# VectorE's order at the start of the first layer: half 0's features and first mask between two parts of the state space weights

## The reference

```
# first sublayer: q, k, v = split(x @ w_attn)
q = elu(q) + 1 ; k = elu(k) + 1                      # the "features"
S_t = S_(t-1) + k_t v_t^T ; z_t = z_(t-1) + k_t
y_t = (q_t S_t) / (q_t . z_t + 1e-6)
x = layernorm(x + y @ w_proj)
# second sublayer holds a state space convolution (64 modes):
dtA = exp(log_dt) * (A_re + i A_im)
dC  = C * (exp(dtA) - 1) / A                         # the "weights"
K   = 2 Re( sum_n dC_n * exp(dtA_n * l) ), l = 0..511  # the taps
```

## Time and profile before

| | |
|---|---|
| runs shown | 670.03, 669.6 and 674.61 us, median 670.03 |
| the profiled execution | 671.23 us |
| its span, first to last instruction | 669.4 us |
| busy in the span | PE 492.3, DVE 438.0, ACT 258.7, POOL 207.8 us |
| mean granted clock of TensorE | 0.851 |
| first block ends on DVE (last row of line 203) | 100.16 us |

### The profile page before, as it was taken

One profiled execution on the slowest core, in us unless ns is written; L12 is line 12 of the kernel. 1 busy time (PEld: TensorE's weight loads), 2 busy tenths in 40 slices (PEclk: granted clock), 3 DMA queues, 4 the chain that ended last, 5 costly groups with the idle time before them and its releaser, 6 DMA issues. The chain is left out here.

```text
span 669.4 us, 11535 instructions
## 1 busy us (share of the span) xinstructions
PE 492.3 (74%) x4041; PEld 357.1 (53%) x4041; DVE 438.0 (65%) x1422; ACT 258.7 (39%) x625; POOL 207.8 (31%) x245
## 2 busy tenths in 40 slices
PE   4597537473599776987768577978598889899960
PEld 2265423361577555776645466756277646455530
DVE  4569896999844777655574998895678554133225
ACT  4499702120013433654113636452266232133321
POOL 3224000553723002655010532330374037044440
PEclk9679955777899886998987677989889879999995
DMA  8100006010000031660000000000735001500012
GB/s 277 43 3 2 1 0 252 9 26 2 0 1 1 0 83 41 114 142 1 1 0 1 2 1 1 1 1 2 290 144 134 2 5 55 138 28 32 29 39 91
DMA packets 28195, 33.44 MB, mean 50 GB/s; under 512 B 5176, under 2 KB 21288, under 8 KB 27625
## 3 DMA queue, kind: packets, MB, share of 16 engines
q1 hardware_dynamic: 26204, 29.24, 14.9%
q0 software_dynamic: 1504, 3.15, 1.4%
q10 hardware_dynamic: 432, 0.33, 0.2%
HBM read 26.50 MB, written 6.21 MB: 49 GB/s over the span
## 5 line engine op out<-in xcount | busy, mean ns | idle before, releaser
L3305 DVE TENSOR_TENSOR em_inner<-banks,em_soft 128x256 f32<-128x256 f32 x31 | 13.1, 424 | 52.5 <-ACT em_soft L3141 52.5
L1777 POOL TENSOR_TENSOR ea_scaled_rows<-ea_scaled_rows 128x768 f32<-128x768 f32 (+2 forms) x24 | 27.7, 1155 | 61.6 <-ACT ea_scaled_rows L1704 60.3
L3189 POOL DMA_INDIRECT em_results<-em_y_slot,slot_rows x31 | 29.7, 957 | 49.7 <-DVE em_y_slot L3313 48.8
L219 ACT ACTIVATE norm_log<-norm_var 128x4 f32<-128x4 f32 x20 | 4.1, 205 | 85.6 <-DVE norm_var L197 85.5
L3079 PE MATMUL banks<-em_up,em_slotT 128*128 x62 | 34.9, 645 | 0.0
L1704 ACT ACTIVATE ea_scaled_rows<-banks,ea_gate 128x192 f32<-128x192 f32 x64 | 23.4, 419 | 25.5 <-PE banks L38 25.4
L2343 POOL TENSOR_TENSOR ga_to_end<-ga_cum 128x512 f32<-128x512 f32 x8 | 12.4, 1545 | 65.1 <-DVE ga_cum L2399 65.0
L1207 POOL TENSOR_TENSOR xa_prob<-xa_score,xa_top 128x308 f32<-128x308 f32 x8 | 5.6, 703 | 75.9 <-DVE xa_left L1304 75.9
L3141 ACT ACTIVATE em_soft<-banks 128x256 f32<-128x256 f32 x31 | 11.9, 383 | 42.7 <-PE banks L3079 42.7
L579 POOL TENSOR_TENSOR lin_q_strip<-lin_qT,lin_strip_head 128x512 f32<-128x512 f32 x8 | 13.9, 1741 | 43.6 <-PE banks L461 29.9
L2738 POOL TENSOR_TENSOR ca_prob<-ca_prob,ca_most 128x1232 f32<-128x1232 f32 x8 | 18.0, 2247 | 19.6 <-DVE ca_most L2791 19.6
(11 more groups left out here) (508 smaller groups left out, 1543.3 us busy)
## 6 DMA issues: line engine op xcount, KB each, us to landing
em_up<-in_em_up SPq DMA_DIRECT2D x3, 1536.0 KB, 11.3
ea_wide<-ea_gates SPq DMA_DIRECT2D x4, 1024.0 KB, 17.0
em_down<-in_em_down SPq DMA_DIRECT2D x3, 768.0 KB, 12.7
em_slots<-slot_rows SPq DMA_DIRECT2D x1, 2108.0 KB, 11.2
w_qkv<-in_w_qkv SPq DMA_DIRECT2D x1, 1536.0 KB, 7.7
slot_rows<-em_slots SPq DMA_DIRECT2D x1, 1360.0 KB, 8.1
cos_lag<-in_cos_lag SPq DMA_DIRECT2D x1, 1024.0 KB, 5.7
sin_lag<-in_sin_lag SPq DMA_DIRECT2D x1, 1024.0 KB, 8.0
```

The lines of the kernel that those rows point to most:

```text
L1777: step(pool.tensor_tensor(scaled_rows[:, k, 0:n], scaled_rows[:, k, 0:n], scaled_rows[:, k, n:2 * n], ALU.add))
L3189: pool.indirect_dma_start(core.results[:, :], bass.IndirectOffsetOnAxis(ap=slot_rows[:, s, P:P + 1].bitcast(U32), axis=0), y_slot[:, s % N ...
```

## The change

On DVE the 25 instructions of `weights` are cut in two. The first 13 (now `steps_to_weights`) stand after `strip_head` and `same_head`. Then come the four feature pieces of half 0 and `mask(0)`, then the other 12 (`weights`), then the four feature pieces of half 1. The loop over the chunks is as it was, and so are the lists of PE, ACT, POOL and SP. No instruction is added or taken away. The wait for the loads of x and the attention parameters (`wait_loaded(dve, "x", "lin")`) now stands ahead of the first 13 instructions, and `step.wait()` behind `same_head` in place of behind the last feature.

```
                 kernel.turns(dve, step)
-                kernel.weights(dve, step)
                 core.wait_loaded(dve, "x", "lin")
                 dve.tensor_reduce(strip_head[:, :], head_of[:, :].rearrange("p (r j) -> p j r", r=STRIPS), AX.X,
                                   ALU.add).then_inc(heads_ready, 1)
...
-                rows = 0
-                for n, (name, dst, _) in enumerate(features):
-                    dve.wait_ge(elu_exp, n + 1)
...
-                        rows += 1
-                        dve.wait_ge(k_rows_relu, rows)
...
                 step.wait()
+                kernel.steps_to_weights(dve, step)
+
+                def features_of(b):
+                    for n in range(4 * b, 4 * b + 4):
+                        name, dst, _ = features[n]
+                        dve.wait_ge(elu_exp, n + 1)
+                        if name[1] != "s":
+                            ring[name].taken(dve)
+                            w = 512
+                        else:
+                            dve.wait_ge(k_rows_relu, 2 * b + n % 4 - 1)
+                            w = 2 * P
+                        dve.scalar_tensor_tensor(dst, exp_of[:, n % 2, 0:w].rearrange("p (a c) -> p a c", c=P), 1.0,
+                                                 relu_of[:, n % 2, 0:w].rearrange("p (a c) -> p a c", c=P),
+                                                 ALU.min, ALU.add).then_inc(elu_done, 1)
...
+                features_of(0)
                 mask(0)
+                kernel.weights(dve, step)
+                features_of(1)
                 for g in range(NT):
...
-    def weights(self, dve, step):
+    def steps_to_weights(self, dve, step):
...
         step(dve.tensor_tensor(ni, ni, q, ALU.add))
+
+    def weights(self, dve, step):
+        are, aim = (self.t["modes"][:, n] for n in (0, 1))
+        em, cm, re, im, nr, ni, q = (self.small[n][:, :] for n in (4, 5, 6, 7, 8, 9, 1))
         step(dve.tensor_tensor(re, are, are, ALU.mult))
```

More of the change, by code:

```diff
@@ L592, in _ @@
                                               spread(head_of[:, :], 2, [P, H, D])))
-                rows = 0
-                for n, (name, dst, _) in enumerate(features):
-                    dve.wait_ge(elu_exp, n + 1)
[L596 to L599, removed]
-                        rows += 1
-                        dve.wait_ge(k_rows_relu, rows)
[L602 to L605, removed]
-                step.wait()
+                step.wait()
+                kernel.steps_to_weights(dve, step)
[12 more added lines that the diff above has]
+                                                 ALU.min, ALU.add).then_inc(elu_done, 1)
                 def mask(g):
@@ L804, in turns @@
         dve.tensor_tensor(small[1][:, :], turn, small[4][:, :], ALU.subtract).then_inc(self.small_fraction, 1)
-    def weights(self, dve, step):
+    def steps_to_weights(self, dve, step):
         dve.wait_ge(self.tanh_ready, 1)
         dve.wait_ge(self.small_sines, 2)
-        are, aim, cre, cim = (self.t["modes"][:, n] for n in range(4))
+        cre, cim = (self.t["modes"][:, n] for n in (2, 3))
         th, sin, half, em, cm, re, im, nr, ni, q = (self.small[n][:, :] for n in (0, 2, 3, 4, 5, 6, 7, 8, 9, 1))
```

## The result

| | kernel before | changed kernel |
|---|---|---|
| runs | 20, median 672.62 us (669.6 to 675.22) | 20, median 669.66 us (667.01 to 675.09) |
| ratio, 95% interval | | 0.9961 (0.9944 to 0.9978) |
| profiled execution | 671.23 us, span 669.4 | 669.62 us, span 667.8 |
| ACT's near turns start | 31.67 us | 27.91 us |
| last layernorm step of the first block ends | 100.16 us | 96.27 us |

The changed kernel is faster by 0.22 to 0.56%, which is 1.5 to 3.8 us. The medians differ by 2.96 us. The forecast was a gain of 4.5 us and a time of 665.5 us, between 661.5 and 669.5; the measured median of 669.66 lies just above that range.

The account below looks back on a forecast made before the run. ACT's unbroken run from the near turns to the first layernorm's root was taken to bound the first block. Strip and head 0, ACT's run 4.5 us earlier, DVE's surplus lost in waits: 670.03 less 4.5, 665.5 us, range 661.5 to 669.5.

Parts of the forecast that it names:

- The chain of the first block: First block: its end follows DVE's tail, ACT's root and ACT's unbroken run from the near turns at 31.67 us.
- Strips and heads ahead of the weights at no cost: DVE's start: strip_head and same_head, 0.36 us, fit into 0.93 us of idle time and cost 0.
- The end of the first score: PE, first block: score starts at 16.41 without a wait, ends at 17.55 or 18.50 us by the clock.
- the case of the end at 18.50: PE's first score at the lower clock, so that half 1's q piece can start at 25.35 us.
- The second rival: First block: a late score 0, at 20.9 us, loses the whole gain, time 670.0; chance 0.07.
- the later blocks, put at nothing on average: Behind the first block: no term in the sum, 1.5 to 2 us either way for the clock.
- the 12 instructions 18.33 - 13.76 = 4.57: DVE, first block: the second part of the weights, behind the first mask, takes 4.57 us.
- the upper case: First score at the upper clock: half 1's q piece at 24.40 us, ACT's near turns 4.78 us earlier.
- over 2 us from 569.2: From the first block's end to the span's end: a rest this far off would show the forecast wrong.
- the third rival: Later blocks' PE clock: 9 us more at the lower level use up the 4.5 us gain; chance 0.08.
- The absolute time: Whole kernel: 665.5 us, from the shown median of 670.03 less the gain of 4.5 us.
- The chances: Whole kernel: within 1% 0.84, faster by over 1% 0.13, slower by over 1% 0.03.

Follow-up runs that it names:

- the two repeats: The kernel before and the changed kernel, each run again without an edit: ratios to the kernel before 0.9986 and 0.9951.
- mask only: Kernel before with only the earlier first mask, all 25 weight instructions ahead of the features again: ratio 1.0015.
- split only: Changed kernel with only the split of the weights kept, first mask behind the features of both halves: ratio 0.989 to the kernel before.
- fourth strip later: Changed kernel with POOL's fourth strip waiting for DVE's eighth feature piece: ratio 0.9941 to the kernel before.
- the three padded ones: Changed kernel with 6, 12 or 24 dead DVE instructions behind the first block's last layernorm: ratios 0.9969, 1.0017, 1.0054 to the kernel before.
- weights late: Changed kernel with the 12 weight instructions moved into DVE's wait ahead of the first far fraction: ratio 0.9894 to the kernel before.
- the root was moved on ACT itself: Weights moved late, plus ACT's first layernorm steps between the 12th and 13th far sizes: ratios 0.9871 and 0.9856 to the kernel before.
- the one of 697.09 us: Profiled execution of the kernel before, run again without an edit: 697.09 us, left out of every ratio.
- padded with 12: Changed kernel with 12 dead DVE instructions behind the first block's last layernorm: ratio 1.0017 to the kernel before.
- the third set: Runs padded with 6 and with 24 and the fastest version again, beside the kernel before at a median of 680.76 us.
- padded with 24: Changed kernel with 24 dead DVE instructions behind the first block's last layernorm: ratio 1.0054 to the kernel before.

## Why the prediction was right and wrong

**The chain of the first block was right.** The forecast read the block's end back to ACT's near turns. In all eleven profiles in which ACT's list was untouched (before, after, the two repeats, mask only, split only, fourth strip later, the three padded ones, weights late) the last layernorm row of the block ended 68.2 to 68.5 us behind the start of the near turns (for instance 27.91 to 96.27 and 23.84 to 92.19). It broke only when the root was moved on ACT itself: 65.4 and 66.7 us. Mask only shows the same from the other side.

**Strips and heads ahead of the weights at no cost: right.** They ran at 8.07 to 8.51, and DVE still waited 0.60 us for ACT's sines.

**The end of the first score: met, but by luck.** It ended at 17.59; I had 17.55 and 18.50 as ends and took 70% of the way to the first. The way there was another. I had PE's k and v rows at the lower level to their end at 16.41 and the score behind them without a wait. The clock rose within these rows, they ended 0.9 us earlier, and the score then waited 0.92 us for the k piece that the strip held. The two cancel. I had also read the earlier trace rows wrongly: in the kernel before, the first five of the eight k and v records took 0.63 us each and the last two 0.38, so there too the clock had risen before 16.41, between 15.4 and 15.8, and 3.09 us is not the pace of the lower level throughout. In all thirteen profiles the last of these records is at the faster pace (0.38 us, 0.44 in the one of 697.09 us): none of them shows the case of the end at 18.50. The second rival, a score that starts near 20.9, is excluded by its start at 16.45. By the Trainium skill (TensorE: Matmul & The Clock Gate, Part 1: The HAM clock gate) the instant of the rise varies between runs: here the trace agrees, since the k and v rows, which began at 13.3 to 13.9 in each profile, took 3.09 us in the kernel before, 2.84 in its repeat, 2.10 after, 1.89 in the repeat of that and 3.15 in the split-only kernel.

**The terms that failed.** The forecast time was 4.2 us too low, and three terms of its sum make that up: the level that the 4.5 was taken from (2.6 us), the first block, whose end moved 3.9 us and not 4.5 (0.6 us), and the later blocks, put at nothing on average, which gave back 0.9 us of the 3.9. The mechanism of the first block held. Each of the three is taken up below.

**The step that failed in the first block: "the 12 instructions 18.33 - 13.76 = 4.57".** They took 5.41. I had used their duration from a place where POOL stood still, and had not counted that the strip of chunk 3, which used to come at 36.70 when DVE was waiting for PE, now becomes free at the end of score 1 in the midst of them. A DVE instruction with two inputs in SBUF that starts just behind a strip is held until the strip has ended. The runs with the strip moved (4.57 us again) and the split-only kernel (another strip, another instruction) show it. The sum then closes: 4.78 of the upper case, less 0.84 for the held instruction, less 0.17 because this execution's loads landed later, is 3.77, and the near turns moved by 3.76. The same hold on the k piece (1.54 us for 0.68) cost less: PE could have started the first score some 0.4 us earlier, when the strip was there (14.81 and half of 2.48 us, an estimate). The two ks pieces behind it took 1.59 us together, and the mask, at 17.83, followed them and not the score, which had ended at 17.59.

**The start of the block varies, and I had taken it as fixed.** ACT's first activation waits for the last load of the state space parameters. It began at 6.49 us in the profile before, at 6.66 in the changed one, and between 6.66 and 7.53 in the others. Everything up to the near turns shifts with it. Counted from there, the near turns come after 25.18, 25.02 and 24.72 us with all 25 weights in front (the last with the earlier mask), after 21.25, 20.85, 20.85, 20.85 and 20.95 in the changed kernel and its padded forms, 20.21 with the strip moved, 18.91 with the split alone and 17.15 to 17.21 with the weights late. So the change is worth some 4.1 us on this stretch (25.1 less 20.95, means of the two profiles before and the five after), where I had 4.5.

**The step that failed behind the first block: the later blocks give back nothing on average.** The sum has no term for them, only 1.5 to 2 us either way in the range, and no row stood behind that; my reason was that most blocks start from a standstill and replay the same sequence. The medians moved by 2.96 and 2.79 us in two sets, for a block end 3.9 and 3.4 us earlier, so 0.9 and 0.6 us were given back. In the profiled pair the span fell by 1.6 us only, and the rest behind the block was 571.5 us where I had named over 2 us from 569.2 as a sign of being wrong. The place of the first part of this loss is visible: the taps' product with the cosines (`taps,cos_lag`) lasted 6.17 us and not 5.47. Its mean granted clock was 0.60 in the changed kernel and 0.68 before. PE's rows, of the kernel before, of the changed one and of its repeat:

```profile
138.55 5.47 PE L1038 MATMUL banks<-taps,cos_lag 128*128 128x128 f32 x32 [2.59 <-issue]
```

```profile
135.18 6.17 PE L1046 MATMUL banks<-taps,cos_lag 128*128 128x128 f32 x32 [3.12 <-issue]
```

```profile
135.26 6.08 PE L1046 MATMUL banks<-taps,cos_lag 128*128 128x128 f32 x32 [3.06 <-issue]
```

DVE's rows in the second block are 3.9 us earlier up to there and 2.7 us behind it. That is the mechanism of the third rival, at a fifth to a quarter of the size that would have turned the sign. It is no chance of one execution. The product took 5.47, 5.39 and 5.19 us (mean granted clock 0.68 to 0.72) in the three profiles whose block ends at 100.3 to 101.1: before, mask only, padded with 12. It took 5.63 to 6.64 us (0.66 to 0.55) in nine others: the changed kernel, its repeat and the other forms. From the second block's first row to the end of the span it is 568.5 to 569.0 us in those three, and 569.3 to 571.8 in the six of the nine that lie outside the third set. As the padding with 12 restores the short product behind an unchanged first block, this points to the time at which the second block starts, and not to something that the changed first block leaves behind. It does not grow with an earlier start, though: the weights-late kernel lost least (5.63 us, block end 92.79), and the kernel padded with 24, whose block ends later than before, has 6.03. One profile of each kernel can't say more, and the medians lose less than the profiles do; what decides where the clock rises against this product is open.

**The absolute time.** 665.5 was 670.03, the median of the three runs shown, less 4.5. Over 20 runs the kernel before has its median at 672.62. That is 2.6 of the 4.2 us by which the forecast time was too low, and more than the mis-sized terms together (1.5 us). Three runs (669.6, 670.03 and 674.61) were too few to take a level from. A gain of 4.5 taken from 672.62 gives 668.1. The chances were right in kind: within 1%, on the faster side.

## What to carry to other kernels

Find the engine whose list has no idle time up to the last wait, and ask of each moved instruction whether it lets that engine start earlier: here the split did, the mask did not and even stood in the way. Work that is read late (the weights, first read at 67.36 us, some 40 us after they are done in the changed kernel) belongs in a wait that its engine has anyway, not ahead of what the bounding engine is waiting for; moved there, it raised the gain from 3 to 8 us. And when instructions of DVE move, look at what POOL will be doing beside them at their new place, and take their duration from rows with such a neighbour.

## What the runs showed of the hardware that was not expected

- A DVE instruction with two SBUF inputs that starts 0.04 to 0.27 us behind a POOL `tensor_tensor` of 128x512 is held until that ends: 1.15 and 1.01 us for 0.29 (the three kernels shown; each ends 0.15 us after the strip), 1.54 for 0.68. The mask, with one input in PSUM, started 0.08 us behind a strip and was not held (2.28 us). When a large DVE instruction with two SBUF inputs is the first, it is POOL that waits: 2.70 us for 1.04, with DVE's 2.28 us unchanged (POOL's row at 38.81 beside DVE's at 38.34 in the changed kernel). The Trainium skill (GPSIMD Engine Reference, 1. Specifications) says that the two engines share their SBUF interfaces and contend where DVE has two SBUF inputs. The trace agrees, and in these rows the one that comes second waits for the end of the first.
- The wait for the first loads varied by 1.04 us between executions (6.49 to 7.53), and a block of 100 us that starts with them varies with it.
- The kernel before had a median of 672.3 us in two sets and 680.76 in the third, which ran on the same chip as the second. Between the profiles of the kernels padded with 12 and with 6 the difference arises late: the rows are level within some 2 us up to 550 us and 7 to 8 us apart from 576 on. In that stretch the same 32 products took 3.81 us in the one, at a granted clock of 1.00, and 5.44 in the other, at 0.69; the eight behind them took 1.04 us in the one and, with gaps between them, 3.25 in the other. What sets this is open.

```profile
563.61 3.81 PE L3024 MATMUL banks<-em_down,em_hidden 128*128 128x128 f32 x32 [1.00 <-DVE em_hidden L3219]
```

```profile
565.04 5.44 PE L3024 MATMUL banks<-em_down,em_hidden 128*128 128x128 f32 x32 [1.99 <-DVE em_hidden L3219]
```
